# Which states GpSimd reads out in the scan of a four-batch Mamba block: states 2, 5, 8, 11 and 14 in place of 3, 7, 11 and 15

## The reference, cut to what matters

```
def step(h, inp):
    dt_t, B_t, C_t, x_t = inp
    dA = jnp.exp(dt_t[:, :, None] * A)
    h = dA * h + (dt_t * x_t)[:, :, None] * B_t[:, None, :]
    y = jnp.einsum('bds,bs->bd', h, C_t)
    return (h, y)
...
y = ys.transpose(1, 0, 2) + xc * D_param
y = y * jax.nn.silu(z)
return jnp.einsum('bld,od->blo', y, out_proj_w)
```

## Time and profile before

| | |
|---|---|
| Median of 3 runs | 2171.52 us (2163.88 to 2172.83) |
| Profiled execution, its own time | 2172.07 us |
| Its span | 2170.1 us |
| Scan phases (first scan to last gate) | four of about 207 us |
| Between phases | about 145 us each |
| Mixture of experts | from about 1500 us on |
| Busy: PE / DVE / POOL / ACT | 76% / 66% / 53% / 40% |

### The profile page before, as it was taken

One profiled execution on the slowest core, in us unless ns is written; L12 is line 12 of the kernel. 1 busy time (PEld: TensorE's weight loads), 2 busy tenths in 40 slices (PEclk: granted clock), 3 DMA queues, 4 the chain that ended last, 5 costly groups with the idle time before them and its releaser, 6 DMA issues. The chain is left out here.

```text
span 2170.1 us, 22230 instructions
## 1 busy us (share of the span) xinstructions
PE 1652.3 (76%) x5692; PEld 922.6 (43%) x5693; DVE 1435.5 (66%) x1492; ACT 868.3 (40%) x1535; POOL 1146.9 (53%) x708
## 2 busy tenths in 40 slices
PE   5357777677778766777778777664699999999990
PEld 2122234342224443222445222344377667666770
DVE  3989996679997858999577999845422222222224
ACT  6535425464432664543456443221122332233223
POOL 2699872569894438988155989500222332233210
PEclk9789998889999888999877999976799999999995
DMA  3075530055561016654004656443011100110107
GB/s 113 6 250 215 202 127 22 5 177 205 194 223 58 5 30 246 208 198 156 23 5 159 212 194 205 185 191 118 24 32 34 34 31 31 34 34 31 31 23 256
DMA packets 76307, 245.72 MB, mean 113 GB/s; under 512 B 10364, under 2 KB 24197, under 8 KB 71366
## 3 DMA queue, kind: packets, MB, share of 16 engines
q1 hardware_dynamic: 69414, 226.17, 29.9%
q0 software_dynamic: 6816, 18.62, 2.7%
HBM read 220.76 MB, written 23.99 MB: 113 GB/s over the span
## 5 line engine op out<-in xcount | busy, mean ns | idle before, releaser
L368 PE MATMUL psum<-HC_sb,ident_sb 128*128 128x512 f32 x1024 | 492.0, 604 | 59.5 <-DVE HC_sb L1320 57.9
L368 PE MATMUL psum<-experts_sb 64*128 64x512 f32 (+4 forms) x962 | 348.3, 572 | 235.9 <-DVE HC_sb L1320 148.1
L913 ACT ACTIVATE psum<-experts_sb 128x1024 f32<-128x1024 f32 x256 | 285.2, 1117 | 476.0 <-DVE experts_sb L1310 387.9
L1310 DVE TENSOR_TENSOR_SCAN experts_sb<-psum,DBX_sb 128x1024 f32<-128x1024 f32 x172 | 390.0, 2277 | 29.6 <-POOL DBX_sb L1017 28.6
L368 PEld LDWEIGHTS psum<-experts_sb 64*128 64x128 f32 (+4 forms) x962 | 116.6, 168 | 495.4 <-DVE HC_sb L1320 242.9
L368 PEld LDWEIGHTS psum<-HC_sb,ident_sb 128*128 128x128 f32 x1024 | 191.1, 192 | 272.7 <-issue 131.5
L1693 ACT ACTIVATE hgt_sb<-psum_moe,b_sb 128x128 f32<-128x128 f32 x568 | 154.3, 382 | 359.3 <-PE psum_moe L1643 359.1
L1606 PE MATMUL psum_moe<-experts_sb,hgt_sb 128*128 x1136 | 259.4, 382 | 4.1 <-ACT hgt_sb L1693 2.6
L1576 POOL DMA_INDIRECT y_rows<-YS_sb,iy_sb x71 | 70.8, 998 | 356.6 <-PE psum_moe L1627 221.7
L1606 PE MATMUL psum_moe<-experts_sb,XGT_sb 128*128 x568 | 257.0, 595 | 0.3 <-issue 0.3
L1606 PEld LDWEIGHTS psum_moe<-experts_sb,hgt_sb 128*128 128x128 f32 x1136 | 216.3, 191 | 66.8 <-issue 40.6
(11 more groups left out here) (248 smaller groups left out, 2179.2 us busy)
## 6 DMA issues: line engine op xcount, KB each, us to landing
DA_sb<-b_rows SPq DMA_DIRECT2D x128, 512.0 KB, 4.8
experts_sb<-b_rows SPq DMA_DIRECT2D x64, 512.0 KB, 3.6
SQ_sb<-b_rows SPq DMA_DIRECT2D x64, 512.0 KB, 4.7
X_XT_sb<-c_rows SPq DMA_DIRECT2D x64, 512.0 KB, 5.5
experts_sb<-w1T SPq DMA_DIRECT2D x8, 1024.0 KB, 19.3
experts_sb<-w2T SPq DMA_DIRECT2D x8, 1024.0 KB, 21.3
experts_sb<-y_rows SPq DMA_DIRECT2D x8, 1024.0 KB, 11.8
X_sb<-x_tok SPq DMA_DIRECT2D x5, 1024.0 KB, 6.9
```

The source lines that it names most:

```text
L368: return nc.tensor.matmul(o, lhsT, rhs, start=start, stop=stop, **k)
L913: nc.scalar.activation(decays[i % 2], DT[:, c, :], ACT.Exp, scale=a_neg[:, s:s + 1]).then_inc(da_ready, 1)
L1310: v.tensor_tensor_scan(STATE[i % STATE_SLOTS], decays[i % 2], DRIVE[i % STATE_SLOTS], 0.0, ALU.mult, ALU.add).then_inc(h_ready, 1)
```

## The change

The list of states whose readout is done by POOL gets five entries in place of four. The distances are three states within a chunk, and four from state 14 of one chunk to state 2 of the next.

```
-POOL_READS = (3, 7, 11, 15)
+POOL_READS = (2, 5, 8, 11, 14)
```

## The result

Before, the median was 2167.70 us (2163.35 to 2172.83, 4 runs), after it 2185.61 us (2184.50 to 2187.17, 4 runs). The ratio is 1.0082 (95% interval 1.0053 to 1.0111): slower by 0.8%. The range of the forecast holds the time, but its likeliest case (+6.4 us, less than the 0.5% that a measurement can tell) is not what happened.

What follows compares the result with a forecast made beforehand. DVE bounds a scan phase by sums, but POOL's later readouts and drives would hold its scans: chunks +0.84, -0.14, +1.74, -0.84 make +1.60 a phase, +6.4 over four, on 2172.07 giving 2178.5 us; range 2164 to 2187.

Steps and rivals of the forecast that it cites:

- third rival: Ends of chunks: DVE's waits make PE's clock fall at every chunk's end, +13 us on the +6.4, 2191 us; chance 0.09.
- Scan i+3 = readout i + 4.75: Scan phase: scan i+3 needs a drive queued behind POOL's readout i, so it starts at least 4.75 us after that readout.
- 9.24 us per three steps: Scan phase: POOL's four instructions per three steps take 9.24 us against DVE's 8.82, so POOL falls 0.42 behind.
- readout 18 at gate + 7.39: Second chunk's start: POOL's first readout waits for PE's sum 16 and starts 7.39 us after gate.
- First chunk: First of a phase's four chunks: scans wait for POOL from step 5 on, gate 0.84 us later than before.
- second rival: Scan phases: DVE's work alone decides, POOL never holds a scan; -18 us over four phases, 2154 us; chance 0.13.
- lag: Start of readout i minus start of scan i; 5.14 us at the second chunk's start, DVE waits once over 4.07.
- the product's term: 8-element product in first_small: 0.2 to 2.3 us in place of 1.6, four times, -6 to +3 us; taken as 0.
- second chunks: Second chunk of each phase, which contains first_small: gate to gate 52.61 us against 52.75 before, -0.14 per phase.
- The third chunk: Third of a phase: PE enters on a slow clock after idling 2.8 us, +1.74 us; at kept speed +0.10.
- The fourth chunk: Last of a phase: readout 63 moves to DVE at 45.85, PE adds until 49.6, gate at 49.65, -0.84 us.
- B rows: Loads: needed after 9.2 us, slowest landed in 5.8, so hidden; rows landing late and slowing the kernel had chance 0.02.

## Why the prediction was wrong where it was

The time lies in the range, near its upper end, and that is in part luck. The end of 2187 us came from the third rival, which did not happen. And the sum started from 2172.07 us, an execution 4.4 us longer than the median of before; from 2167.70 the same +6.4 gives 2174.1, where 2185.61 was measured: +17.9, nearly three times the forecast.

**What held.** Scan i+3 = readout i + 4.75 (4.76 measured); 9.24 us per three steps; readout 18 at gate + 7.39; each waiting scan 0.3 to 0.4. First chunk +0.84 forecast, +0.82 measured in the second phase. POOL does decide over DVE's work, so the second rival fell as argued: five readouts take work off DVE that it then spends waiting, until the readouts start at state 3 with a lag of 2.6.

**What failed: the product's term.** The step read "it may now meet POOL's instructions elsewhere: from 0.2 to 2.3 us in place of 1.6, four times ... I take 0". It took 4.7, outside both ends, and 4 x 3.1 = 12.4 us is most of the error (second chunks: 12.0 measured, -0.6 forecast). The upper end of 2.3 is one POOL instruction: it took for granted, without a row, that the product gets in when the POOL instruction beside it ends. In the trace of before it had been so in all four phases. Its timeline of POOL and DVE at this place, which the prediction did not read:

```profile
572.75 2.35 POOL L1017 TENSOR_TENSOR DBX_sb<-experts_sb 128x1024 f32<-128x1024 f32 x1
...
573.53 1.59 DVE L1070 TENSOR_TENSOR experts_sb<-experts_sb 128x8 f32<-128x8 f32 x1
...
575.06 2.34 POOL L1017 TENSOR_TENSOR SQ_sb<-SQ_sb,experts_sb 128x1024 f32<-128x1024 f32 x1
```

The product came in drive 34 and was through at 575.12, when that drive ended (575.10); behind it only drive 35 could go. The Trainium skill has a rule on it (SBUF — State Buffer, SBUF: two separate sides): of a GpSimd instruction and a DVE instruction with two SBUF inputs, whichever starts first has the shared ports for its whole instruction, and the other is blocked. That section says nothing on who comes next. If the waiting one did, the wait would be one POOL instruction at most; 53 of the 82 products below agree, 29 took longer.

**What the long case has in common.** In seven profiles of changed kernels, 82 such products ran beside a busy POOL. In 32 the two POOL instructions next in line were drives whose inputs were there when the product came (three of these came within 0.02 us of such a drive's start, and I count that drive as next): 28 of them took 4.66 us or more, until both drives were through. In the other 50 only one drive was ready, or a readout stood first in line: 49 took under 2 us, until the running instruction's end. So by this pattern the second cause is the lag again. In the kernel before, where POOL keeps up, the product meets drive 34; with POOL later it meets drive 33, or readout 31, with 34 and 35 ready, and the small product waits for both. This is a rule read off the runs, with two breaches: the four pairs behind step 41 had two ready drives before them and took 1.1, and the one of 4.25 had not. The pattern was found in these profiles and not tested by a run of its own. Why an instruction passes POOL's boundary in one case and not in the other stays open.

**The third chunk.** Forecast +1.74, measured +2.04. The choice of the slow clock was right, for a reason that was not mine: by the working PE would have been idle for 2.8 us, and it was 5.93, by the product. With the product out of the way it is 1.52 and the clock stays. The step chose between bounds of 1.45 and 3.20 us, and the other traces narrow them. All 123 of PE's blocks that came after 1.4 to 1.9 us of idle time, over the thirteen profiles, ran at a granted clock of 1.00. One block came after 2.60 us (products behind other chunk starts, fourth phase). Its row and its busy time and clock:

```profile
1342.19 5.72 PE L368 MATMUL psum<-experts_sb 128*64 128x512 f32 x10 [2.60 <-DVE experts_sb L1327]
1342.10:1345.40 3.30, 3.21 (x4) 0.75 (x4) 3.27 (x2) 0.00 (x0) 1.33 (x1) 0.51 0.66 228
```

So the 2.8 us of the working would most likely have met the slow clock too, but that is one case.

**The fourth chunk.** Forecast -0.84, measured -1.28: gate stood at + 49.21 where 49.65 was worked out. The terms up to readout 63 hold (scan 62 at + 39.86, readout 63 at + 45.78 where 45.85 was worked out). PE then ended the sum of step 63 at + 49.18, not at 49.6: its last sum stands 0.4 us closer behind the readout than the working had it.

**B rows.** "Hidden, with 3.4 us of room", and the earlier load "costs nothing": the mechanism was listed with 0.02 and its price was real. Two readings failed. The 5.8 us of the earlier trace rows was the maximum of 30 loads of one phase; in its fourth phase the same trace has a row that landed after 7.6 us and held POOL:

```profile
1189.10 2.35 POOL L1017 TENSOR_TENSOR DBX_sb<-DA_sb,experts_sb 128x1024 f32<-128x1024 f32 x1 [0.91 <-DMA DA_sb<-b_rows]
```

And the room was not 9.2 us everywhere. "Always one readout among them" does not hold for the row of step 4: only drives 1, 2 and 3 stand between its issue and its use, 6.7 us. The row of step 3 waits for no drive and goes out as the phase starts; in the changed kernel's third phase it was needed after 5.8 us. With the load issued at step 2, POOL waited for a B row in 11 of 28 profiled phases (seven kernels), at step 3 in 7 of 20 (five kernels, the one before among them), in halves at steps 4 and 7 in none of 4. With readouts at 3, 7, 11 and 15 these waits cost the chunk nothing. In the changed kernel the one wait cost 2.9 us (56.65 against 53.80 in the second phase).

**The chances.** The sum of +6.4 us with 10.9 us as what a measurement can tell made "no change" the likeliest. The missing 12.4 us of the product took it across, and the late row added 2.9; a gain of the fifth readout was 0.13 in the second rival, for a reason (POOL never holds a scan) that the waits of 0.33 refute.

## What to carry to other kernels

An engine that has room in the sum can still hold another, if its first instruction of a stretch starts late: work out the lag at the start of each stretch, not only the rates. A tiny instruction with two SBUF inputs beside a busy POOL is not priced by its size, and not by one POOL instruction either: look at how many of POOL's next instructions are ready (the pattern found here, not a tested rule), and put it where POOL waits for something (here two steps later, worth 0.5% by itself). Small loads that are needed soon should not be issued right behind a large one on the same queue: count the room from issue to use at the start of each stretch, and place or split the large one so that the tight loads go first.

## What the runs showed of the hardware

- DVE's 128x8 product with both inputs in SBUF took 0.15 to 0.17 us with POOL idle, up to 1.94 until the running POOL instruction's end, and 4.7 to 5.6 us in 28 of 32 cases when two ready drives stood behind that one. Scans (one input in SBUF, one in PSUM) stayed at 2.26 to 2.29 us with POOL busy 192 of 224 us.
- A 512 KB load behind a 1 MB load on SP's queue landed in 8.0 to 9.6 us in the four phases of the changed kernel, against medians of 4.3 to 4.6.
- PE's block ran at a granted clock of 0.50 after 5.93 us of idle time and took 6.11 us; after 2.60 us it ran at 0.51 and took 5.72 (once); after 1.52 us it ran at 1.00 and took 4.16.
